# The last feed-forward's slots: the new batch's products first, the token copy last

## The reference, cut to what matters

```
x_diff = x[:, None] - select_mean_diff[None, :, None]
x_diff = x_diff / norm(x_diff, axis=3)
score  = (einsum('nds,bntd->bnts', select_weight, x_diff) ** 2).sum(-1)
gate   = sigmoid(imp_slope * (score - imp_center))
sel_scale, sel_idx = gate.max(axis=1), gate.argmax(axis=1)
mod_x  = einsum('btdh,btd->bth', lora_update[sel_idx], x - debias_w[sel_idx])
out    = (1 - sel_scale) * x + sel_scale * (bias_w[sel_idx] + einsum('btdh,bth->btd', lora_degen[sel_idx], mod_x))
```

## Time and profile before

| | |
|---|---|
| median of 3 runs | 2024.15 us (2023.63 to 2030.39) |
| profiled execution | 2028.65 us, of which the span of the records 2026.9 us |
| busy share of the span | PE 88%, DVE 67%, POOL 44%, ACT 37% |
| mean granted TensorE clock | 0.952 |
| this stage | 1860.8 us to the end, 166 us |

### The profile page before, as it was taken

How to read it: one execution, slowest core, us unless ns; L and a number is a source line. 1 busy time by engine, 2 the same in 40 slices (tenths; PEclk the granted TensorE clock), 3 DMA queues, 4 the chain that set the end, 5 groups by cost and what they waited for, 6 DMA issues and landing times.

```text
span 2026.9 us, 41093 instructions
## 1 busy us (share of the span) xinstructions
PE 1786.1 (88%) x14072; PEld 1263.6 (62%) x14072; DVE 1352.0 (67%) x3592; ACT 744.1 (37%) x1511; POOL 900.6 (44%) x965
## 2 busy tenths in 40 slices
PE   8999999689998799999999888999877878998776
PEld 5555555389997455555555556677655666886443
DVE  4676777455554566666666667888845776886765
ACT  2444444222222355556565641111122222443332
POOL 0254545566555254545464543332343223664333
PEclk9999999899999799999999999999998887999887
DMA  5300000000003655454545400000011000000111
GB/s 182 110 6 6 7 5 9 10 31 9 10 8 71 140 102 107 94 109 91 111 89 114 87 7 14 9 10 8 9 37 42 13 16 17 14 16 14 33 38 49
DMA packets 68405, 93.86 MB, mean 46 GB/s; under 512 B 10168, under 2 KB 62504, under 8 KB 64936
## 3 DMA queue, kind: packets, MB, share of 16 engines
q1 hardware_dynamic: 68280, 92.15, 19.8%
HBM read 61.84 MB, written 29.49 MB: 45 GB/s over the span
## 4 chain that ended last, share of the span: by engine, by line
PE 67%; DVE 16%; issue 6%; ACT 5%; POOL 2%; DMA 2%; SPq 1%; DVEq 1%; ACTq 0%; POOLq 0%
PE PS L1039 16%; PE PS L2031 3%; PE PS L687 3%; PE PS L1206 3%; PE PS L1995 3%; DVE negmax L2359 3%; PE PS L744 3%; PE PS L2121 3%; PE PS L520 2%; PE PS L760 2%; ACT pw L2274 2%; PE PS L741 2%; PE PS L711 2%; PE PS L2056 1%; PE PS L788 1%
## 5 line engine op out<-in xcount | busy, mean ns | idle before, releaser
L2359 DVE TENSOR_REDUCE negmax<-PS 128x2 f32<-128x512 f32 (+1 forms) x384 | 247.1, 685 | 167.2 <-PE PS L2031 161.2
L551 POOL TENSOR_TENSOR X<-X,y_sb 128x512 f32 (+1 forms) x128 | 163.6, 1278 | 147.8 <-DVE y_sb L546 142.8
L546 DVE TENSOR_TENSOR y_sb<-PS,ga_sb 128x512 f32<-128x512 f32 x96 | 66.3, 690 | 180.9 <-PE PS L1039 50.4
L1039 PE MATMUL PS<-we_hi,h_parts 128*128 128x512 f32 x512 | 177.4, 407 | 1.7 <-POOL h_parts L1488 1.6
L530 ACT ACTIVATE hT<-PS,modT 128x256 f32<-128x256 f32 x256 | 130.5, 562 | 111.5 <-PE PS L520 110.5
L2274 ACT ACTIVATE pw<-PS 128x512 f32<-128x512 f32 x256 | 139.2, 600 | 73.2 <-PE PS L2031 73.2
L510 DVE TENSOR_SCALAR xn<-X,mv,rs 128x256 f32 (+1 forms) x256 | 153.5, 641 | 5.7 <-POOL rs L503 3.6
L501 POOL TENSOR_TENSOR rs<-mv,eps 128x2 f32<-128x2 f32 x128 | 26.7, 209 | 285.3 <-DVE mv L494 285.1
L1039 PE MATMUL PS<-l_h_parts,lut_hi 128*128 128x256 f32 (+1 forms) x768 | 144.4, 290 | 6.7 <-POOL l_h_parts L1172 6.7
L1039 PEld LDWEIGHTS PS<-l_h_parts,lut_hi 128*128 128x128 f32 (+1 forms) x768 | 116.7, 183 | 9.7 <-issue 5.4
L1582 DVE SCALAR_TENSOR_TENSOR l_acc<-PS,rt_g,l_acc 128x256 f32<-128x256 f32 x256 | 105.9, 475 | 21.1 <-PE PS L1039 20.9
(11 more groups left out here) (280 smaller groups left out, 4295.5 us busy)
## 6 DMA issues: line engine op xcount, KB each, us to landing
ga_sb<-ga_dram SPq DMA_DIRECT2D x128, 128.0 KB, 2.9
qk_dram<-qk_parts SPq DMA_DIRECT2D x64, 192.0 KB, 2.8
KS<-qk_dram SPq DMA_DIRECT2D x32, 384.0 KB, 5.7
QS<-qk_dram SPq DMA_DIRECT2D x32, 384.0 KB, 9.0
qk_dram<-qk_parts SPq DMA_DIRECT2D x64, 128.0 KB, 2.8
wmod<-in_wmod SPq DMA_DIRECT2D x4, 1536.0 KB, 13.6
qk_dram<-qk_parts SPq DMA_DIRECT2D x64, 64.0 KB, 2.5
y_out<-X SPq DMA_DIRECT2D x16, 256.0 KB, 2.2
```

Of the source, the lines that this page charges most:

```text
L551: pool.tensor_tensor(xb(b), xb(b), y_sb[b.par][:, :, :], ALU.add).then_inc(s.x.sem, 1)
L1039: last_ = pe.matmul(out, x.bitcast(F32R), y.bitcast(F32R), start=start and n == 0, stop=stop and n == 2)
L2359: dve.tensor_reduce(to, src, AX.X, ALU.max, negate=True).then_inc(s.max.sem, 1)
```

## The change: what it does

Only the order inside `slot` is changed, on three engines; no instruction is added or dropped. GpSimd and SyncE keep their order.

- TensorE before: `rows_T(i-1)`, `wide_gates_T(i-2)`, `products(i)`, `tokens(i)`, transposes of i+1, `norms(i)`, `out(i-2)`. After: `products(i)`, `wide_gates_T(i-2)`, `rows_T(i-1)`, transposes of i+1, `out(i-2)`, `norms(i)`, `tokens(i)`.
- ScalarE before: `l_hsq(i)`, exponential of i-1, `l_sq(i)`, `l_mx(i)`, `l_ht(i)`, `l_rows(i)`, modulate of i+1. After: `l_hsq(i)`, `l_sq(i)`, `l_mx(i)`, exponential of i-1, modulate of i+1, `l_rows(i)`, `l_ht(i)`.
- VectorE before: `ratio(i-1)`, apply of i+1, `l_zz(i-2)`, `choice(i-1)`, `l_y(i-2)`, statistics of i+2. After: apply of i+1, statistics of i+2, `l_zz(i-2)`, `ratio(i-1)`, `l_y(i-2)`, `choice(i-1)`.

```diff
--- before.py
+++ after.py
@@ -1777,18 +1777,18 @@
                 last_.then_inc(s.y_ps.sem, 1)
 
             def slot(i):
+                if i.ok:
+                    products(i)
+                if (i - 2).ok:
+                    wide_gates_T(i - 2)
                 if (i - 1).ok:
                     rows_T(i - 1)
-                if (i - 2).ok:
-                    wide_gates_T(i - 2)
-                if i.ok:
-                    products(i)
-                    tokens(i)
                 ahead(ln_transpose, pe, pl, i, 1)
-                if i.ok:
-                    norms(i)
                 if (i - 2).ok:
                     out(i - 2)
+                if i.ok:
+                    norms(i)
+                    tokens(i)
 
             slots(pe, slot, -1, (4, 14), B + 1)
 
@@ -1797,15 +1797,12 @@
             act.wait_ge(setup["f_set"], 1)
 
             def slot(i):
+                p = PS[:, l3f_bank(i), :]
                 if i.ok:
                     act.wait_ge(*s.h(i))
                     if (i - 1).ok:
                         act.wait_ge(*s.p_ps(i - 1))
                     act.activation(l3_hsq[:, :, :], hT[i.par][:, :, :], ACT.Square).then_inc(s.hsq.sem, 1)
-                if (i - 1).ok:
-                    route_exp(act, pl, s, i - 1)
-                if i.ok:
-                    p = PS[:, l3f_bank(i), :]
                     act.wait_ge(*s.p_ps(i))
                     if (i - 1).ok:
                         act.wait_ge(*s.s_ps(i - 1))
@@ -1813,16 +1810,19 @@
                     if (i - 2).ok:
                         act.wait_ge(*s.zz(i - 2))
                     act.activation(l3_mx[i.par][:, :], p[0:NS + E, T:2 * T], ACT.Identity, bias=l3_c0[:, 0:1]).then_inc(s.mx.sem, 1)
-                    act.wait_ge(*s.hfree(i))
-                    if (i - 2).ok:
-                        act.wait_ge(*s.y1(i - 2))
-                    act.activation(l3_ht[i.par][:, :, :].rearrange("p t d -> p (t d)"), bank(2), ACT.Copy).then_inc(s.ht.sem, 1)
+                if (i - 1).ok:
+                    route_exp(act, pl, s, i - 1)
+                ahead(modulate, act, pl, i, 1)
+                if i.ok:
                     act.wait_ge(*s.s_ps(i))
                     if (i - 1).ok:
                         act.wait_ge(*s.zT_ps(i - 1))
                     act.activation(l3_rows[:, :], p[0:ROWS, 0:T], ACT.Identity, bias=l3_rowb[:, 0:1],
                                    scale=l3_roww[:, 0:1]).then_inc(s.z.sem, 1)
-                ahead(modulate, act, pl, i, 1)
+                    act.wait_ge(*s.hfree(i))
+                    if (i - 2).ok:
+                        act.wait_ge(*s.y1(i - 2))
+                    act.activation(l3_ht[i.par][:, :, :].rearrange("p t d -> p (t d)"), bank(2), ACT.Copy).then_inc(s.ht.sem, 1)
 
             slots(act, slot, -1, (4, 14), B)
 
@@ -1883,9 +1883,8 @@
                 last_.then_inc(s.g.sem, 1)
 
             def slot(i):
-                if (i - 1).ok:
-                    ratio(i - 1)
                 ahead(ln_apply, dve, pl, i, 1)
+                ahead(ln_stats, dve, pl, i, 2)
                 if (i - 2).ok:
                     b = i - 2
                     dve.wait_ge(*s.gT_ps(b))
@@ -1893,7 +1892,7 @@
                         dve.wait_ge(*s.y_ps(b - 1))
                     dve.tensor_tensor(l3_zz[:, :], PS[0:NS + E, 6, 0:T], l3_mx[b.par][:, :], ALU.mult).then_inc(s.zz.sem, 1)
                 if (i - 1).ok:
-                    choice(i - 1)
+                    ratio(i - 1)
                 if (i - 2).ok:
                     b = i - 2
                     dve.wait_ge(*s.y_ps(b))
@@ -1902,7 +1901,8 @@
                     for t in range(TT):
                         dve.scalar_tensor_tensor(l3_y1[:, t, :], l3_ht[b.par][:, t, :], l3_oms[b.par][:, t:t + 1],
                                                  bank(4)[:, t * D:(t + 1) * D], ALU.mult, ALU.add).then_inc(s.y1.sem, 1)
-                ahead(ln_stats, dve, pl, i, 2)
+                if (i - 1).ok:
+                    choice(i - 1)
 
             slots(dve, slot, -2, (4, 14), B + 1)
```

More of the change, by code:

```diff
@@ L1779, in slot @@
             def slot(i):
+                if i.ok:
+                    products(i)
+                if (i - 2).ok:
+                    wide_gates_T(i - 2)
                 if (i - 1).ok:
                     rows_T(i - 1)
+                ahead(ln_transpose, pe, pl, i, 1)
                 if (i - 2).ok:
-                    wide_gates_T(i - 2)
-                if i.ok:
-                    products(i)
-                    tokens(i)
-                ahead(ln_transpose, pe, pl, i, 1)
+                    out(i - 2)
                 if i.ok:
                     norms(i)
-                if (i - 2).ok:
-                    out(i - 2)
+                    tokens(i)
             slots(pe, slot, -1, (4, 14), B + 1)
```

## The result

The changed kernel took 1999.13 us (median of 4 runs, 1995.8 to 2004.52) against 2023.89 us for the kernel before (4 runs). The ratio of the two is 0.9874, with a 95% interval of 0.9843 to 0.9904: faster, by 24.8 us. The forecast was 2001 us, 22.9 less. The profiled execution went from 2028.65 us (span 2026.9) to 1999.81 us (span 1998.0).

What follows compares the result with a forecast made beforehand. A ring through TensorE, VectorE and ScalarE bounds each slot; VectorE becomes the bound. 24.5 + 3.9 - 5.5 = 22.9 us less, from 2024.15 to 2001 us; range 1994 to 2008 (0.68).

Steps and rivals of the forecast that it cites:

- First three slots: Slots 0 to 2, before the first steady products: 18.4 us instead of 22.3, 3.9 less, said to hold no gates or `l_y`.
- Steady slot: Slots 3 to 14: 8.05 us each on VectorE instead of 10.09, together 24.5 us less.
- The stalls: VectorE's `choice` waits beside GpSimd: L1396 0.7 us for the gate, L1399 0.9 for the addition to `x`; 1.6 a slot.
- The wait for `out`: On VectorE, `l_y(i-2)` waits for TensorE's `out(i-2)`, partly covered by `ratio`: adds 0.35 us a slot.
- The 0.2 for `ln_rstd` beside `ratio`: GpSimd's `ln_rstd(i+2)` running beside VectorE's `ratio` might hold up L1860: between nothing and 0.7 us a slot, 0.2 taken.
- The end: From products(15) to the end of the kernel: 28.3 us instead of 22.8, 5.5 more.
- The clock: TensorE's clock stays at 1.00 in steady slots, products 3.1 us, because its idle gaps fall below 1.69 us.
- the ring through ScalarE's copy: In each old slot `out`, `l_y`, ScalarE's token copy, `l_rows`, modulate, then products: 10.09 us, TensorE idle 2.28.
- Rival 1: `choice` takes no stall and TensorE bounds the slot at 6.5 us: 45 us less, 1979 us; chance 0.10.
- Rival 2: TensorE's clock still falls in the steady slots, 9.6 us each: 3 us less, 2021 us; chance 0.11.
- Rival 3: VectorE waits out all GpSimd work and `out` runs at low clock, slot 10.6 us: 8 more, 2032 us; chance 0.05.
- rival 4: The slot is bound elsewhere, such as a buffer wait, and stays 9.5 to 10 us: about 2020 us; chance 0.06.

Runs made afterwards that it cites:

- the small gate: The changed kernel with GpSimd's two gate instructions cut to 8 of 256 features per token: 1977.98 us, ratio 0.9746.
- the first filling: The kernel before with three products of constants on 72 rows of the array added behind `out` in each slot: 2030.83 us, ratio 1.0005.
- the later one: The changed kernel run again unaltered, on one chip with ScalarE's order alone and the gate a slot later: 2000.34 us, ratio 0.9843.
- the two fillings: The kernel before with products of constants behind `out`: three on 72 rows, 2030.83 us, ratio 1.0005; four on 128 rows, 2002.76 us, ratio 0.9876.

## Why the prediction was right

- **The sum**: the total of 22.9 us lies near the 24.8 of the medians, but its terms measure 4.3 (first slots), 28.3 (12 slots) and -3.8 (end), 28.7 together, in the profiled executions from which they were worked out. The forecast was 5.8 us short there, mostly by the length of the slot. That the median agrees better than the terms is luck.
- **First three slots**: forecast 18.4 us, measured 17.98. "No gates or `l_y` are in them" was a misreading: in the trace of before, slot 2 has `out(0)` at 1878.97 and `l_y(0)` at 1880.07 on its chain, and is 8.56 us long for it. In the new order they hold nothing up (slot 2 is 5.97 us), so the sum came out all the same.
- **Steady slot**: forecast 8.05, measured 7.73 over the 12. VectorE is the bound, as argued. The stalls were forecast at 0.7 (L1396) and 0.9 (L1399), and are 0.6 to 0.8 and 0.85, where the small gate shows that they are GpSimd's. The wait for `out` was taken as 0.35 and is 0.57 to 0.6: `ratio` covers the 0.85 that I had counted, but `out` starts 0.55 us behind the start of `l_zz` (1922.44, 1922.99), as it needs its end and signal, and I had taken the 0.34 to VectorE's next start. The 0.2 for `ln_rstd` beside `ratio` was wrong: L1860 takes 0.17 while L503 runs. The stream itself was summed from single durations and is some 0.25 us shorter, as an instruction starts a little before the one ahead has ended (apply 0.65 to the next start, not 0.73; `l_y` 0.79, not 0.88).
- **The end**: 28.3 forecast, 26.6 measured. `l_zz(13)` starts 3.8 us behind the last products and not 5.4, and what follows it has about the length forecast. Its long rounds through `choice`, gates, `l_zz` and `out` at the low clock are there:

```profile
1988.61 0.64 PE L1741 MATMUL PS<-ident,l_g 128*72 128x128 f32 x2 [4.29 <-DVE l_g L1881]
...
1989.76 2.07 PE L1776 MATMUL PS<-l_dg,l_zz 72*128 72x256 f32 x4 [0.51 <-DVE l_zz L1893]
```

- **The clock**: the forecast of full clock held in all steady slots but two (0.98 over 1890 to 1960). The first low phase fell on `out` (1.70 us instead of 1.13) and made its slot 8.33 us long; the second fell behind `out` and cost VectorE nothing. The reason given, that the length of TensorE's idle gap decides (1.69 us keeps the clock, 2.28 loses it), is refuted by the first filling, where 0.92 us lost it in each slot, and by the changed kernel itself, which lost it twice after gaps of 0.67 us. That the step came out right is therefore partly luck. What differs between the two fillings is the rows in use (72 against 128), the number of weight loads (6 against 8) and the constants multiplied, at equal busy time and equal columns moved; which of these it is stays open.
- **What carries the gain**: the prediction named the ring through ScalarE's copy, but summed up three engines' orders together and did not say which of them is needed. Shown: ScalarE's order alone gives all of it, TensorE's and VectorE's without it give a loss of 0.64%, and TensorE's and ScalarE's without VectorE's give nothing.
- **Rival 1** (6.5 us a slot without stalls) was sized well: 6.25 with the small gate. **Rival 2** (the clock still falls) came about in two slots of this trace and three of the later one, at 0.5 us or nothing each. **Rival 3** (VectorE's ring over 10.09 us) and **rival 4** (9.5 to 10 us, bound elsewhere) didn't: the slot is 7.73. No run shows rival 3's price.

The Trainium skill, page "SBUF — State Buffer", section "SBUF: two separate sides", calls the port pair an exclusive lock between GpSimd and VectorE instructions with two SBUF inputs or in a two-port mode. The small gate agrees (0.94 and 1.02 us back to 0.17 and 0.18), as do `l_y` and the statistics, with one SBUF input each and no stall beside GpSimd. L1860 does not: it has two SBUF inputs and takes 0.17 us in the middle of L503, which reads SBUF too. There the measurement decides.

## What to carry to other kernels

Look for the ring before moving work: here one copy at the wrong place of one engine's stream held back the next slot, and one engine's order was enough. Put behind the instruction that releases GpSimd what ran beside it at its usual length (here the statistics, and `l_y`, which takes one input from PSUM), or let GpSimd work a slot later. And read the granted clock beside the idle gap without taking the gap for its cause: test it with a filling. Last, compare the length of the changed stage in the traces beside the medians of the whole kernel: here two versions with the same ratio differ by 10 us in the stage.

## What was not expected of the hardware

- Equal gaps, different clocks: 0.92 us idle and 1.46 us of products on 72 rows left the low phase in each slot; 0.97 us idle and 1.47 us of products on 128 rows removed it. In the changed kernel it came twice after 0.67 us idle.
- A GpSimd instruction of 0.71 us on two columns (L503) did not hold up a VectorE instruction with two SBUF inputs (L1860, 0.17 us), where one of 1.27 us on 512 columns held up L1396 for 0.6 to 0.8. In the run with the gate a slot later L1396 and L1397, with two SBUF inputs as well, take 0.18 each beside L503.
- The slots of the kernel before and of the first filling are equally long (10.24 us on average), although TensorE has 1.46 us more to do in the second, and their low phases come in the same place.
